# When a second batch's context is turned: ahead of the first attention step, or within it

## The reference, cut to what matters

```python
x = x + _L0_xattn_ref(_layernorm(x), ctx_1024, ctx_1024, w_q, w_k, w_v, w_o)   # x (2,256,256), ctx (2,4096,256)

def _L0_xattn_ref(query, key, value, w_q, w_k, w_v, w_o):      # 16 heads of 64
    q = (query @ w_q).reshape(B, Q, HEADS, HEAD_DIM).transpose(0, 2, 1, 3)
    k = (key @ w_k).reshape(B, Kl, HEADS, HEAD_DIM).transpose(0, 2, 1, 3)
    v = (value @ w_v).reshape(B, Kl, HEADS, HEAD_DIM).transpose(0, 2, 1, 3)
    scores = jnp.einsum('bhqd,bhkd->bhqk', q, k) * scale
    attn = jax.nn.softmax(scores, axis=-1)
    out = jnp.einsum('bhqk,bhkd->bhqd', attn, v)
    return out.transpose(0, 2, 1, 3).reshape(B, Q, HEADS * HEAD_DIM) @ w_o
```

## Time and profile before

| what | us |
|---|---|
| median of 3 runs | 1198.45 |
| lowest, highest | 1192.63, 1201.44 |
| the profiled execution, its own time | 1196.23 |
| its span, first to last instruction | 1194.5 |
| start of step one's scores | 74.52 |
| row maximum for step two copied (ACT L1448) | 129.59 |

### The profile page before, as it was taken

One profiled execution on the slowest core, in us unless ns is written; L12 is line 12 of the kernel. 1 busy time (PEld: TensorE's weight loads), 2 busy tenths in 40 slices (PEclk: granted clock), 3 DMA queues, 4 the chain that ended last, 5 costly groups with the idle time before them and its releaser, 6 DMA issues.

```text
span 1194.5 us, 33355 instructions
## 1 busy us (share of the span) xinstructions
PE 1081.4 (91%) x13853; PEld 787.5 (66%) x13853; DVE 817.8 (68%) x1184; ACT 898.3 (75%) x1624; POOL 691.9 (58%) x605
## 2 busy tenths in 40 slices
PE   5779999999999999999999999999999878637698
PEld 3456777777777777677767676777777766413455
DVE  4978686777777686868686868686777454857322
ACT  4768888787888888888878788888787874479533
POOL 4476666666666666666666666666666771235023
PEclk9999999999999999999999999999999989856679
DMA  6310111101010101010101010111102400000000
GB/s 227 112 36 20 37 37 26 46 22 38 19 38 19 37 19 38 19 37 20 37 19 37 20 37 20 37 37 27 40 20 59 143 2 2 1 0 1 1 1 18
DMA packets 28391, 42.00 MB, mean 35 GB/s; under 512 B 2618, under 2 KB 23122, under 8 KB 27218
## 3 DMA queue, kind: packets, MB, share of 16 engines
q1 hardware_dynamic: 28242, 39.88, 12.0%
HBM read 22.57 MB, written 0.52 MB: 19 GB/s over the span
## 4 chain that ended last, share of the span: by engine, by line
PE 76%; DVE 9%; ACT 8%; issue 4%; POOL 2%; DMA 0%; DVEq 0%; ACTq 0%; POOLq 0%
PE ps L1223 13%; PE ps L1237 12%; PE ps L1298 8%; PE ps L1300 8%; PE ps L1315 6%; PE ps L1257 6%; PE ps L1320 5%; PE ps L1318 4%; DVE m_part L1607 2%; PE ps L684 2%; PE ps L702 2%; ACT probs L1472 2%; PE ps L1283 1%; PE ps L1199 1%; POOL psums L1770 1%
## 5 line engine op out<-in xcount | busy, mean ns | idle before, releaser
L1770 POOL TENSOR_TENSOR psums<-probs 128x512 f16<-128x512 f32 x512 | 592.9, 1169 | 314.0 <-ACT probs L1472 177.1
L1472 ACT ACTIVATE probs<-ps 128x512 f32<-128x512 f32 x512 | 305.2, 600 | 51.8 <-PE ps L1300 51.2
L1607 DVE TENSOR_REDUCE m_part<-ps 128x2 f32<-128x1024 f32 x256 | 311.8, 1221 | 28.3 <-PE ps L1257 25.5
L1298 PE MATMUL ps<-q,k 128*128 128x256 f16 x1024 | 252.0, 273 | 7.0 <-ACT probs L1472 5.8
L1315 PE MATMUL ps<-v_sb,probs 128*128 128x65 f16 x2048 | 242.2, 194 | 15.1 <-issue 9.1
L1300 PE MATMUL ps<-q,k 128*128 128x256 f16 x1024 | 251.8, 273 | 0.0
L1470 ACT ACTIVATE probs<-ps 128x512 f16<-128x512 f32 x384 | 229.3, 597 | 21.9 <-PE ps L1300 18.0
L1318 PE MATMUL ps<-v_sb,probs 128*128 128x64 f16 x2048 | 240.2, 193 | 0.0
L1320 PE MATMUL ps<-v_sb,psums 128*128 128x65 f16 x2048 | 239.2, 194 | 0.0
L1315 PEld LDWEIGHTS ps<-v_sb,probs 128*128 128x128 f16 x2048 | 188.9, 98 | 69.2 <-issue 40.7
L1597 DVE TENSOR_TENSOR k<-ps,k 64x512 f16<-64x512 f32 x256 | 176.2, 688 | 53.5 <-ACT k L1429 49.4
(11 more groups left out here) (203 smaller groups left out, 1645.5 us busy)
## 6 DMA issues: line engine op xcount, KB each, us to landing
k<-k SPq DMA_DIRECT2D x64, 256.0 KB, 3.6
probs<-in_ctx_dram SPq DMA_DIRECT2D x4, 1024.0 KB, 5.2
k<-in_ctx_dram SPq DMA_DIRECT2D x4, 1024.0 KB, 6.2
k<-in_L_ffn_W_dram SPq DMA_DIRECT2D x2, 2048.0 KB, 11.5
wqk_raw<-in_L_xattn_w_q_dram SPq DMA_DIRECT2D x16, 128.0 KB, 3.6
wqk_raw<-in_L_xattn_w_k_dram SPq DMA_DIRECT2D x16, 128.0 KB, 3.4
wv_raw<-in_L_xattn_w_v_dram SPq DMA_DIRECT2D x16, 128.0 KB, 3.1
wo_raw<-in_L_xattn_w_o_dram SPq DMA_DIRECT2D x16, 128.0 KB, 2.8
```

Source lines behind the costliest of these rows:

```text
L1298: pe.matmul(ps[:, SC + s % 2, cols], k1[:, par, h, keys], q1[:, par, h, :], start=True, stop=False)
L1472: nc.scalar.activation(p_raw[:, s % NX, :, :], scored, ACT.Exp, scale=XSCALE) \
L1607: nc.vector.tensor_reduce(m_part[:, j, t, :], ps[:, bank:bank + 2, :], AX.X, ALU.max) \
L1770: nc.gpsimd.tensor_tensor(p_lo[:, s % NP, :, :].rearrange("p h q -> p (h q)"), p_raw[:, s % NX, :, :].rearrange("p h q -> p (h q)"), p_hi[ ...
```

## The change

Ahead of step one only ten units are prepared: the eight of batch 0 and the first two of batch 1 (`EARLY`). The other six units of batch 1 are prepared in step one, in twelve halves (`LATER_AT`: slot, then unit and feature half). A half is four transposes into bank `PM` (`transposes_later`), a copy by ACT and a subtraction by DVE (`context_later`); the next half waits for the subtraction (`s_cl`). The first waits for the low part of q of step two (`s_ql`), which uses the same bank, and step two's key chunks wait for their unit.

In the prologue a unit's two banks are now read in one instruction each: ACT copies both as `ctx_hi` (128x1024), copies both again in fp32 to `copies`, and POOL makes both low parts. DVE has no part in it. Each round has one unit instead of two; key chunk `j` is projected with its low-part product last, so that only the last two of six matmuls wait for POOL. The first split of key weights comes ahead of the normalisation on both ACT and DVE. Value chunk 2 is projected after `max_rows`, and waits for DVE's part of value chunk 0.

The loads of context are all issued at the start: eight of 512 tokens for batch 0 into `stage`, and for batch 1 two pieces a unit straight into `ctx_hi` and `ctx_lo` of batch 1, each unit one place further on than where its turned form will lie (the last one into a new buffer, `last_raw`). POOL fills the `k2` rows of batch 0 at the start (two instructions) and those of batch 1 in slots 6, 12, 18 and 24 of step one (four instructions of 64x2048), for which step two waits; DVE's `row_vectors` moves to slot 24.

```diff
+TURNED = 2
+EARLY = 2
+ROWS_AT = (6, 12, 18, 24)
+LATER_AT = {1: (2, 0), 2: (2, 1), 4: (3, 0), 6: (3, 1), 7: (4, 0), 9: (4, 1), 11: (5, 0), 13: (5, 1),
+            15: (6, 0), 17: (6, 1), 19: (7, 0), 20: (7, 1)}
...
+            for u in range(KCH):
+                for i in range(2):
+                    to = last_raw[:, 2 * i:2 * i + 2, :] if u == KCH - 1 else raw1[i][:, :, u + 1, :]
+                    first = 4 * (u % 2) + 2 * i
+                    sp.dma_start(to, chunks[1, u // 2, :, first:first + 2, :]).then_inc(s_raw[u], 16)
...
+            def transposes_later(k, u, c):
+
+                if c == 0:
+                    pe.wait_ge(s_raw[u], 32)
+                if k == 0:
+                    pe.wait_ge(s_ql, 2)
+                else:
+                    pe.wait_ge(s_cl, k)
+                turn_context(1, u, c, PM).then_inc(s_cx, 1)
...
+                if n == 1 and j >= EARLY and 0 in halves:
+                    pe.wait_ge(s_cl, 2 * (j - EARLY) + 2)
...
+            def project_first_k(j, bank):
...
+                products = [(w, y, c) for w, y in ((wk_hi, ctx_hi), (wk_lo, ctx_hi), (wk_hi, ctx_lo))
+                            for c in range(NC)]
+                for i, (w, y, c) in enumerate(products):
+                    if i == 0:
+                        pe.wait_ge(s_th, j + 1)
+                    if i == 4:
+                        pe.wait_ge(s_tl, j + 1)
+                    mm = pe.matmul(ps[:, bank, :], w[:, 0, c, :], y[:, 0, c, keys],
+                                   start=(i == 0), stop=(i == 5))
+                mm.then_inc(s_k, 1)
...
+            for j in range(2, KCH + 2):
+                transposes_ctx(j)
+                if j < KCH + 1:
+                    at_least(pe, s_kl, j - 2)
+                    project_first_k(j - 1, (PV, PK)[(j - 1) % 2])
+                else:
+                    pe.wait_ge(s_kl, KCH - 1)
+                    project_v(0, 0, 0, PV)
+                maxima(2 * (j - 2), 0, 0)
+                maxima(2 * (j - 2) + 1, 0, 0)
+            pe.wait_ge(s_kl, KCH)
+            project_v(1, 0, 0, PK)
+            pe.wait_ge(s_th, KCH + EARLY)
             max_rows(0)
+            pe.wait_ge(s_vl, 1)
+            project_v(2, 0, 0, PV)
...
+            def context(i):
+                b, _, keys = context_part(i)
+                act.wait_ge(s_tp, i + 1)
+                nc.scalar.activation(ctx_hi[:, b, :, keys], ps[:, TURNED:TURNED + 2, :], ACT.Copy)
+                at_least(act, s_tl, i - 1)
+                nc.scalar.activation(copies[:, i % 2, :, :], ps[:, TURNED:TURNED + 2, :], ACT.Copy) \
+                    .then_inc(s_th, 1)
+
+            def context_later(k, u, c):
+                act.wait_ge(s_cx, k + 1)
+                nc.scalar.activation(ctx_hi[:, 1, c, 512 * u:512 * (u + 1)], ps[:, PM, :], ACT.Copy) \
+                    .then_inc(s_ch, 1)
...
+                    if first and s in LATER_AT:
+                        context_later(list(LATER_AT).index(s), *LATER_AT[s])
```

More of the change, by code:

```diff
@@ L220, in perceiver @@
         s_x = sem("s_x")
-        s_ctx = [sem(f"s_ctx{i}") for i in range(4)]
+        s_ctx = [sem(f"s_ctx{i}") for i in range(KCH)]
+        s_raw = [sem(f"s_raw{i}") for i in range(KCH)]
         s_wqk = [sem("s_wqk0"), sem("s_wqk1")]
@@ L1449, in take_max @@
                                      scale=1.0 / MS).then_inc(s_mr, 1)
-            def context(u):
-                b, _, _, keys = context_pair(u)
-                for c in range(NC):
-                    act.wait_ge(s_tp, 2 * u + c + 1)
-                    i = nc.scalar.activation(ctx_hi[:, b, c, keys], ps[:, TURNED[c], :], ACT.Copy)
-                    if c == 1:
-                        if u >= 4:
-                            act.wait_ge(s_tl[1], u - 3)
-                        i = nc.scalar.activation(copies[:, u % 4, :], ps[:, TURNED[c], :], ACT.Copy)
-                    i.then_inc(s_th, 1)
+            def context(i):
[9 more added lines that the diff above has]
+                    .then_inc(s_ch, 1)
             def step(hp, b):
@@ L1605, in maxima @@
                     at_least(dve, s_mn, n)
-                bank = SC if isinstance(n, int) and n == 0 and t == 1 else MX
+                bank = MX if n or t == 0 else SC
                 nc.vector.tensor_reduce(m_part[:, j, t, :], ps[:, bank:bank + 2, :], AX.X, ALU.max) \
@@ L1671, in step @@
                         split_p(slot_of(hp, b, s), s)
+                    if s == 24 and first:
+                        dve.wait_ge(s_const, 5)
+                        row_vectors(dve)
                     if s == Q_AT and more:
@@ L1699, in _ @@
             dve.wait_ge(s_mz, 2)
[L1700 to L1715 removed]
+            dve.wait_ge(s_x, 16)
+            variance(0, slice(0, NT))
+            split_k(0, 0)
+            normalised(0, slice(0, NT))
+            for j in range(1, KCH + 2):
                 if j >= 2:
                     maxima(2 * (j - 2), 0)
+                if j == 5:
+                    split_v(0, 0)
+                if j == 6:
+                    split_k(1, 1)
+                if j < KCH + 1:
+                    take_k(j - 1, 0, 0, (PV, PK)[(j - 1) % 2])
+                if j == 1:
+                    take_q(0, 0)
+                if j >= 2:
                     maxima(2 * (j - 2) + 1, 0)
[L1719 removed]
+            take_max(0)
+            for j in range(AHEAD):
                 take_v(j, 0, (PV, PK)[j % 2])
[L1721 to L1723 removed]
             for hp in range(HP):
```

222 lines of the change are left out of this document (100 added, 122 removed).

## The result

The changed kernel takes **1189.84 us** (median of twenty; 1187.52 to 1193.59) against 1198.05 us of the kernel before timed beside it: ratio 0.9939, 95% interval 0.9923 to 0.9955, so 8.2 us or 0.6% less. The forecast was 5.7 us less, 1192.7. Within 1% it is the same; the sign is shown. One of the twenty executions fell into the chip's slow state (1279.46 us at a granted clock of 0.82) and is in neither the range nor the ratio.

What follows compares the result with a forecast made beforehand. TensorE was taken to bound a steady step and VectorE the prologue ahead of step one. A 16.0 us earlier start less 10.3 us given back in step one made -5.7 us: 1192.7 from the median 1198.45, range 1186 to 1201.

Steps and rivals of the forecast that it cites:

- Rounds: Prologue rounds: VectorE, rid of context work, stays the bound at 3.85 us a round instead of 5.27.
- rival A: Prologue rounds: ScalarE, GpSimd and TensorE take turns instead of overlapping, 4.4 to 4.5 a round, +4 us, 1196.7; 15%.
- long ring: Prologue rounds: turns, ScalarE's reads, GpSimd, last projection matmuls and maxima in sequence, 7.1 us for two rounds, 3.55 each.
- Opening: Start of the prologue: x ready 0.8 us later, first maximum at 25.6, last maximum done at 56.0.
- Rival B: Opening chain of the prologue: TensorE's clock rises as late as before, costing +2.5 us, 1195.2; 12%.
- Hand-over: Between last maximum and step one: scores start at 58.5 instead of 74.52, a gain of 16.0 us.
- Step one: Step one takes back work of six units: 10.3 us longer than 55.1, bounds 7 and 17.
- The handshakes: Step one: later half units wait for ScalarE and VectorE to read their one bank, 1.5 us in all.
- Loads: Context loads, all issued at the start: covered by the opening chain, put at zero.
- fills: Step one: GpSimd's four fills each hold a VectorE cast, +6.4 us, 1199.1, no change; 5%.
- single bank: Step one: each later half unit waits 2.35 us like the first, 24 us more, 1217; 6% beyond 1201.
- Handshakes free and opening shorter: Step one and prologue: handshakes cost nothing, opening a microsecond shorter, -9 us, 1189.5; 15%.

Runs made afterwards that it cites:

- the later pair: The changed kernel and the kernel before, timed again later without an edit: 1191.4 and 1198.39 us, ratio 0.9953.
- e2: The changed kernel with its first four later halves in slots 3, 4, 5 and 6 instead of 1, 2, 4 and 6: 1188.91 us.
- e11: The changed kernel with its first load delayed by one more GpSimd fill, about 1.8 us, nothing else moved: 1192.04 us.
- e5: The changed kernel with a small unused exponential added on ScalarE, so the table load comes before the hand-over: 1189.97 us.
- e8: The changed kernel with each later half turned twice, the first result thrown away: 1196.47 us in one run.
- e1: The changed kernel with the row vectors put back ahead of step one instead of in slot 24: 1190.23 us.
- e6: The changed kernel with the row vectors in slot 30 of step one instead of 24: 1185.63 us over five runs.
- e12: The changed kernel with loads of batch 0's units 4 to 7, and batch 1's behind them, held until earlier turns ended: 1190.67 us.
- e9: The changed kernel once more, without an edit, for a second profile and more runs: 1191.4 us.
- e10: The kernel before once more, without an edit, for a second profile: one run of 1199.25 us.

## Why the prediction was right, point by point

The forecast held in its sign, its class and its range; it was 2.5 us short of 8.2 in the medians (1.3 short of the 7.0 of the later pair). Against the profiles of the head it was 3.5 short (5.7 of 9.21), and the terms show where.

1. **Rounds.** Right: 3.81 a round without splits (forecast 3.85), VectorE the bound. GpSimd's 1024 columns take 2.13 (taken as 2.3), ScalarE's pair 2.04. No other ring sets them, so rival A is out. (The terms of the long ring add to 7.0, not 7.1, and the last sum of part 2 takes 0.3 for seams where 0.2 is named; neither changes the forecast.) The busy share was 94.6%, where above 95% was named.
2. **Opening.** The mis-sized term. x was turned at 12.14 (forecast 13.1, before 12.25), and TensorE came to its full pace at 16 us, not at 23. The forecast moved the old normalisation by 0.8 and kept its length. It did start 0.72 later, but in the kernel before one of its four instructions had been held up by GpSimd's first low part, and in the changed kernel that comes later. The kernel before (beside 9.98 2.21 in the earlier trace rows), then the changed kernel:

```profile
10.48 1.25 POOL L1752 TENSOR_TENSOR ctx_lo<-psums,ctx_hi 128x512 f16<-128x512 f32 x1 [1.88 <-ACT psums L1459]
```

```profile
10.70 1.38 DVE L1610 TENSOR_SCALAR xn<-x_sb,mv,rstd 128x256 f32<-128x256 f32 x4
...
11.99 2.12 POOL L1805 TENSOR_TENSOR ctx_lo<-psums,ctx_hi 128x1024 f16<-128x1024 f32 x1 [3.23 <-ACT psums L1507]
```

   So 0.8 us of the opening hang on when the context lands: in e2 the two met again, and x was turned 1.81 later. The prediction weighed such a hold for the casts of step one only. The first maximum ran at 22.85 instead of 25.6, 2.75 earlier. Of this 0.9 went back by the last maximum (54.14 instead of 56.0), part of it to the lower stretch at 42 us (e11 without it: from the turns at 41.11 to the scores 15.93; the changed kernel from those at 39.73: 16.65, so 0.7; e2 and e5, without it too, also take 30.6 from the first maximum to the end of the last, the changed kernel 31.3). Rival B was out in the other direction: half of the opening's work is turns, and the pace rose all the same.
3. **Hand-over.** Right by its own terms: last maximum ends at 54.14, scores at 56.38, 2.2 apart (forecast 2.5). The gain was 18.1 instead of 16.0 through point 2.
4. **Step one.** 8.93 instead of 10.3. The turns: 12 x 0.43 = 5.2 instead of 6.4; the 1.06 of eight turns in the earlier trace rows holds the way of the last one through the engine, which a full stream hides (e8 shows it once more). The first wait: 4.82 in slot 1 where 1.35 stood before, less 0.43 of turns, so 3.0 (forecast 2.35), for the right reason; e2 and e5 show that ScalarE, late by the value chunk and the table load, is its root. The second: 0.6 (0.4). The clock: slot 0 from 3.37 to 1.95, -1.4 (-0.8), at a granted clock of 0.66 between 74.5 and 79.5 us before and 1.00 between 56.4 and 60 now. The handshakes: slots 7, 13, 20 and 21 together 0.5 (1.5). The row vectors: 1.1 (0.5 with the fills), shown by e1 and e6, by way of a maximum. Sum 5.2 + 3.0 + 0.6 - 1.4 + 0.5 + 1.1 = 9.0.
5. **Loads.** Zero within the slack that e12 tries.

The two large errors, 2.1 us in the opening and 1.4 in step one, have the same sign and do not cancel. Why the medians show 8.2 and 7.0 and not the 9.2 of the head stays open: falls of the clock in step one (2.3 us in e9) and the tail can both have a part in it.

The rival of the **fills** (D) did not come, but it wasn't put to the test: the four fills took 1.80 each at 73.6, 84.2, 97.6 and 108.6, and none of the eight casts lay beside one. Maxima that did took 1.22, as always. The **single bank** (E): three waits of 0.8 in all; e8 doubled the load on it and found TensorE's own time in seven of the twelve slots. **Handshakes free and opening shorter** (C, -9, 1189.5) has the number nearest to the median, and half of its mechanism: the opening was shorter, the handshakes cost 0.5. What stays open is when exactly the clock falls or rises in a stretch like the one behind the first turns; four against three executions tell no rule.

## What to carry to other kernels

Work that is moved out of a prologue bound by one engine into a step bound by another is paid in the step at the successive starts of its instructions in the stream (0.43 us for four turns), not at their duration alone (0.53), and in the waits at the seam: there, look for what is already late on the engine that must pass it on (here a table load and a value chunk) before moving the work itself. A side job on a nearly full engine costs by its place, not by its length: the same row vectors cost 1.1 in slot 24, where they took 2.6 us, and nothing in slot 30, where they took 4.8. Before a difference of a few us is explained, profile the same kernel twice: unchanged code differed by 3.6 us here between two executions of one kernel, and by 7.7 over fourteen profiles.

## What the hardware showed unexpectedly

- (Timeline of TensorE, the kernel before, below.) TensorE came to its full pace at 16 us in the changed kernel, 4 us after x's turns began without a gap; in the kernel before, with the same turns at 12.25 and waits of 1.18 and 2.09 us behind them, eight turns at 25.55 still took 1.86, and only those at 28.68 took 1.07:

```profile
21.26 1.94 PE L1190 MATMUL ps<-ident,probs 128*128 128x128 f32 x8 [2.09 <-DVE ctx_lo L1620]
...
25.55 1.86 PE L1190 MATMUL ps<-ident,k 128*128 128x128 f32 x8
```

  In e10 the turns at 25.57 took 1.64 and the next 1.06. Over the twelve profiles of the new opening the full pace came between 15 and 20 us, 3 to 6 us after x's turns began; in e1 it came within the second pair of key matmuls (14.76, 0.81 us), 1 us after the first instruction of the execution that is no turn (13.90). About half of the work in either opening is turns. The Trainium skill (TensorE: Matmul & The Clock Gate, Part 4: PE-mode transpose) says that turns do not count for the clock in the same way; the rows show that they did not keep it down here.
- The granted-clock column reads 1.00 for the stretch 10 to 15 us in which eight turns take 1.97; later stretches at that pace (64 to 68 us in e9) read 0.50. Early in an execution the pace is to be read from durations.
- The executions of one kernel fall into groups by mean granted clock: of the changed kernel's later twelve, five at 0.951 or 0.952 took 1188.0 to 1189.9 and seven at 0.944 to 0.948 took 1190.6 to 1195.6; the kernel before has 1190.8 at 0.958, 1194.2 at 0.960, 1197.9 to 1200.8 at 0.949 and 1201.5 at 0.945. Two medians a few us apart need many runs.
- A 128x1 VectorE instruction took 1.13 us instead of 0.16 beside a GpSimd subtraction (e1), and in e6 three of them took 0.60, 1.02 and 1.02, each to the subtraction's end.
- An earlier landing of the context made the opening longer: turns of it at 7.17 instead of 7.92 put GpSimd's low part beside the normalisation, and the scores came 1.84 later (e2).
